# An order of steps rewritten: the quantised layer within the cross attention before it, and the first causal scores at its end

## What is computed

```
x6 = x5 + attention(norm(x5), ctx)                 # third layer: cross attention, 16 heads of 8, 77 keys
q  = clip(round(norm(x6) / s), -128, 127)          # s = max(|norm(x6)|) / 127 per token
x7 = x6 + (q @ weight_q.T) * s * weight_scale + bias      # quantised layer
y  = norm(x7)                                      # input of a decoder of four layers:
for l in range(4):                                 #   l = 0 begins here
    q, k, v = split(rmsnorm(y) @ Wqkv.T + b)       #   rope on q and k
    y += causal_attention(q, k, v) @ Wo.T + bo     #   512 x 512 scores, 16 heads of 8
    y += cross_attention(rmsnorm(y), ctx)          #   masked by token segments
    y += silu(h @ Wg.T) * (h @ Wu.T) @ Wd.T        #   h = rmsnorm(y)
x8 = x7 + rmsnorm(y)
```

## Time and profile before

| | us |
|---|---|
| median of 3 runs | 2295.73 |
| lowest and highest | 2293.84, 2301.45 |
| the profiled execution | 2289.95 |
| its span in the profile | 2288.2 |
| PE, DVE, ACT, POOL busy | 1928.6, 1443.6, 1072.7, 634.6 |
| mean granted clock of PE | 0.914 of full |

### The profile page before, as it was taken

The page is one execution under the profiler, slowest core; times in us unless marked ns, Lnnn a source line. Parts: engine busy times, 40 slices in busy tenths (PEclk is TensorE's granted clock), DMA queues, the critical chain, the costliest instruction groups (busy, mean ns, idle before and its releaser), DMA issues.

```text
span 2288.2 us, 33985 instructions
## 1 busy us (share of the span) xinstructions
PE 1928.6 (84%) x13195; PEld 1171.1 (51%) x13195; DVE 1443.6 (63%) x3533; ACT 1072.7 (47%) x1517; POOL 634.6 (28%) x858
## 2 busy tenths in 40 slices
PE   5977999675772899999889899889999989989977
PEld 4556565364541444565544465544455544456553
DVE  7546655553666777754577774477775457776468
ACT  2542555221451566454366555256645446645510
POOL 1111000322423444200354310245420144421020
PEclk9988999677785899899899899999989989989988
DMA  7001000121000000000000000000000000000000
GB/s 248 14 1 56 1 1 12 33 76 49 23 1 12 1 1 1 1 10 12 14 1 1 1 11 1 26 1 1 1 1 10 1 14 2 1 1 10 1 1 19
DMA packets 26929, 38.60 MB, mean 17 GB/s; under 512 B 5384, under 2 KB 20112, under 8 KB 26128
## 3 DMA queue, kind: packets, MB, share of 16 engines
q1 hardware_dynamic: 24720, 32.23, 4.3%
q0 software_dynamic: 2048, 4.20, 0.6%
HBM read 25.93 MB, written 10.49 MB: 16 GB/s over the span
## 4 chain that ended last, share of the span: by engine, by line
PE 45%; DVE 12%; ACT 6%; issue 4%; POOL 1%; DVEq 0%; POOLq 0%; ACTq 0%
PE wide L681 33%; PE acc L681 13%; DVE maxima L1587 4%; ACT prob L1829 3%; DVE hid L1109 1%; POOL rstd L1887 1%; DVE x L1648 1%; ACT prob L1752 1%; DVE moments L1142 1%; DVE hid L1266 1%; DVE qkv L1555 1%; ACT hn L1717 1%; DVE maxima L1275 1%; DVE hn L1187 1%; ACT q_g L1673 0%
## 5 line engine op out<-in xcount | busy, mean ns | idle before, releaser
L1587 DVE TENSOR_REDUCE maxima<-wide 128x2 f32<-128x512 f32 (+3 forms) x512 | 407.3, 819 | 167.5 <-PE wide L681 164.0
L1829 ACT ACTIVATE prob<-wide 128x768 f32<-128x768 f32 (+1 forms) x384 | 331.4, 881 | 140.4 <-PE wide L681 140.1
L1752 ACT ACTIVATE prob<-wide 77x1024 f32<-77x1024 f32 x256 | 260.2, 1019 | 150.5 <-PE wide L681 150.3
L1275 DVE TENSOR_REDUCE maxima<-wide 128x8 f32<-128x616 f32 x256 | 202.9, 795 | 174.4 <-PE wide L681 172.8
L681 PE MATMUL wide<-q_g 32*128 32x256 f32 (+3 forms) x2048 | 273.8, 403 | 33.9 <-ACT prob L1829 18.5
L2030 POOL TENSOR_SCALAR_AFFINE_SELECT prob<-prob 128x256 f32<-128x256 f32 (+1 forms) x384 | 186.5, 490 | 353.7 <-ACT prob L1829 351.2
L681 PE MATMUL wide<-q_g,kx 128*77 128x512 f32 x512 | 258.0, 576 | 3.2 <-DVE hid L1513 2.0
L1887 POOL TENSOR_TENSOR rstd<-moments,cst 128x4 f32<-128x4 f32 x88 | 89.9, 1021 | 580.9 <-DVE moments L1163 282.4
L681 PEld LDWEIGHTS wide<-q_g 32*128 32x128 f32 x2048 | 141.4, 192 | 209.5 <-issue 116.7
L1673 ACT ACTIVATE q_g<-wide 128x1024 fp32r<-128x1024 f32 x128 | 131.2, 1025 | 212.2 <-PE wide L681 212.2
L1673 ACT ACTIVATE q_g<-acc 128x512 fp32r<-128x512 f32 x192 | 114.5, 597 | 178.4 <-PE acc L681 178.0
(11 more groups left out here) (228 smaller groups left out, 3141.8 us busy)
## 6 DMA issues: line engine op xcount, KB each, us to landing
A<-in_w SPq DMA_DIRECT2D x2, 2048.0 KB, 12.9
unit_w<-in_unit_w SPq DMA_DIRECT2D x8, 448.0 KB, 3.4
ffn_w<-in_ffn_w SPq DMA_DIRECT2D x4, 768.0 KB, 4.3
slots_in<-f2x SPq DMA_DIRECT2D x1, 2560.0 KB, 23.8
prob<-slots_in SPq DMA_DIRECT2D x8, 320.0 KB, 3.1
slots_out<-A SPq DMA_DIRECT2D x8, 320.0 KB, 2.2
...
```

Source lines behind the costliest of these rows:

```text
L1275: e.tensor_reduce(maxima[g % 2][:, 2 * half:2 * half + 2, :], v, AX.X, ALU.max, negate=True).then_inc(*made("max", ("free", tile)))
L1587: e.tensor_reduce(top[:, t, h], v[:, :, at0:at0 + P * t + P], AX.X, ALU.max, negate=True).then_inc(*made("max", *([("free", tile)] if t == ...
L1752: e.activation(p[0:SC, :], s[0:SC, :], ACT.Exp, bias=0.0, scale=1.0).then_inc(*made("exp", pb, ("free", tile)))
L1829: e.activation(pv, sv, ACT.Exp, bias=0.0, scale=8 ** -0.5).then_inc(*made("exp", pb, ("free", tile)))
```

## The change

1. `clear` is cut in nine pieces (CLEARS): eight memsets of 640 columns of A and a last piece with the rest. They lie beside the scores of entry 1 of the third layer.
2. The quantised layer of entries 0 and 1 is put within the third layer's items: `stats`, `apply` and the three parts of `quantise` at the end of the phase of finish(b), and `turn`, `f2_matmul`, `stats` and `apply` of "in" in one phase more. For entry 0 `begin` of the first decoder layer follows in that phase, and `rotate`, `cut_q` and `cut_k` in another.
3. The quantised layer of entries 2 and 3 gets two phases that lie beside the causal attention's items, and so do the masks (masks3 beside item 5, mask_turn beside item 6, counted from 0).
4. `quantise` is the same nine instructions, now in three steps; f2_matmul's product has two buffers of its own (f2_hid).

```diff
+    def quantised(b):
+        quantise = [("quantise", b, k) for k in range(3)]
+        if b > 1:
+            return [[[]]] * b + [
+                in_rows((3, ("stats", "f2", 0, b)), (5, ("apply", "f2", 0, b)), *zip((7, 9, 11), quantise)),
+                in_rows((1, ("turn", "f2", 0, b)), (3, ("f2_matmul", b)), (6, ("stats", "in", 0, b)), (10, ("apply", "in", 0, b)))]
+        head = [[("stats", "f2", 0, b)], [("apply", "f2", 0, b)] + quantise]
+        tail = [[], [], [("turn", "f2", 0, b)], [("f2_matmul", b)], [("stats", "in", 0, b)], [("apply", "in", 0, b)]]
+        if b:
+            return [head, tail]
+        tail += [[("stats", "s", 0, b), ("variance", "s", 0, b)], [("apply", "s", 0, b)], [], [("turn", "s", 0, b)],
+                 [("qkv", 0, b, 0)], [("qkv", 0, b, 1), ("bias_o", 0)]]
+        return [head, tail, [[("rotate", 0, b, k)] for k in range(6)] + [[("cut_q", 0, b)], [("cut_k", 0, b)]]]
+
+    if n == 3:
+        items = [[prepare(b), scores(b), attend(b)] for b in range(B)]
+        items[1][1] = beside(items[1][1], [[("clear", k)] for k in range(CLEARS)])
+        for b, item in enumerate(items):
+            more = quantised(b)
+            item += [finish(b) + more[0]] + more[1:]
+        return items
...
     def prepare(b, g):
+        if (l, b, g) == (0, 0, 0):
+            return in_rows((11, ("qk_turn", l, b, g)))
+        if (l, b) == (0, 0) and g < 3:
+
+            return beside(in_rows((8, ("qk_turn", l, b, g))),
+                          in_rows((0, ("stats", "s", l, 1)), (2, ("variance", "s", l, 1)), (4, ("apply", "s", l, 1)),
+                                  (8, ("turn", "s", l, 1)), (10, ("qkv", l, 1, 0)), (12, ("qkv", l, 1, 1)))
+                          if g == 1 else rotate(1, *[(k, 3 * k) for k in range(5)]))
...
-    items = [[[[("stats", "f2", 0, b)], [("apply", "f2", 0, b), ("quantise", b)], [], [], [("turn", "f2", 0, b)]],
-              [[("f2_matmul", b)]], [[("stats", "in", 0, b)], [("apply", "in", 0, b)]]] for b in range(B)]
-    items[0][0] = beside(items[0][0], [[("clear",)]])
-    every += items
     for l in range(NL):
         project, rotate, items = self_steps(l)
-        every[-1] = [beside(every[-1][0], project)] + every[-1][1:]
         if l == 0:
-            items[1][0] = beside(items[1][0], [[("masks3", k)] for k in range(4)] + [[], [], [("mask_turn", "l3")]])
-        every += [rotate] + items + cross_steps(4 + l) + [[[]]]
+            items[5][0] = beside(items[5][0], in_rows(*[(3 * k, ("masks3", k)) for k in range(4)]))
+            items[6][0] = beside(items[6][0], in_rows((5, ("mask_turn", "l3"))))
+            every.append([[]])
+        else:
+            every[-1] = [beside(every[-1][0], project)] + every[-1][1:]
+            every.append(rotate)
+        every += items + cross_steps(4 + l) + [[[]]]
```

61 lines of the change are left out of this document (34 added, 27 removed).

## The result

| | runs | median us | lowest to highest |
|---|---|---|---|
| before | 10 | 2301.22 | 2289.36 to 2311.89 |
| after | 10 | 2281.72 | 2277.18 to 2294.56 |

The ratio is 0.9932, with a 95% interval of 0.9911 to 0.9953: the change makes the kernel faster by 0.7%, some 15.6 us (the two medians lie 19.5 us apart). The forecast was 31.3 us, twice what the ratio gives. The direction held, and the time lies inside the range of 2249 to 2283, near its upper end. The profiled execution of after is the slowest of its ten (2294.56 us, span 2292.8, granted clock 0.907), that of before (2289.95, 0.914) is about as fast as the fastest of its ten (2289.36), so the two profiles must not be compared by their spans, but stretch by stretch.

The account below looks back on a forecast made before the run. PE paced the causal items; ahead of them PE waited for DVE and POOL, whose chain ran in series. Terms of -55.3, +22.5 and +1.5 gave -31.3 us, from 2295.73 to 2264.4, range 2249 to 2283.

Parts of the forecast that it names:

- The main term: Ahead of the causal attention: the first causal maximum starts at 695.5 and not at 750.8, -55.3 us.
- the chain's last one: Entry 0's chain beside entry 3's attend, up to the first causal maximum: 26 us, with 20 or 32 possible.
- no wait of PE for a maximum is above 4 us: Sign near 640 us, around the scores of entries 2 and 3: no PE wait above 4 us there.
- entry 3's logits don't start near 669: Sign ahead of entry 3's attend: its logits would start near 669, as before.
- The failing step: Causal attention's items 0 to 4, now carrying moved DVE work: 82.9 us together against 60.4, +22.5.
- the masks' turn: mask_turn beside a full causal item, where PE has no idle time that covers it: +1.5 us.
- POOL: Items 1 to 4: DVE's instructions slowed beside POOL's work, taken at 3, 1, 1 and 1 us.
- The segments' wait: Item 4: DVE stands some 4 us for the segments' load, with entry 1's maxima queued behind.
- the sum: Whole kernel: -55.3, +22.5 and +1.5 give -31.3 us, from 2295.73 to 2264.4 us.
- the port rival: Causal items: all 28 moved DVE instructions cost 0.98 us extra each beside POOL, whole time 2285; chance 0.12.
- My rival: From 640 us to the sixth item: PE's clock stays at 1.2 GHz, +59 us if throughout; chance 0.05.
- the 0.8 at which I said I would be wrong: Sign in the causal items: the prediction is wrong if PE's clock there falls under 0.8.

Follow-up runs that it names:

- experiment 4: Three edits of the changed kernel: entry 1's rotation on POOL shrunk, rounding and clipping of entries 2 and 3 left out, and both; ratios 0.9928, 0.9930, 0.9926 to before.
- e10: Changed kernel with the clear as one whole memset again, at its new place beside entry 1's scores; ratio 0.9922 to the kernel before.
- experiment 6: Variants of the changed kernel with the quantised layer of entries 2 and 3 and the masks placed in other items; ratios 0.9856 to 0.9935 to before.
- e6: Changed kernel with the causal logits' products of items 1 to 5 issued twice; ratio 0.9955 to the kernel before.
- e15: Changed kernel with an own buffer for the segments, the masks over items 7 to 10 and their turn beside item 11; ratio 0.9935 to before.
- e7: Changed kernel with entry 1's rotation on POOL shrunk to 128x8 blocks; ratio 0.9928 to the kernel before.
- e5: Changed kernel, segments' own buffer, entry 2's quantised layer from the cross attention's end to item 1, entry 3's over items 2 to 5, masks over 7 to 10; ratio 0.9868.
- e11: As e5, with the masks put back into items 3 and 4 and their turn beside item 5; ratio 0.9856 to the kernel before.
- e3: Changed kernel, segments' own buffer, entry 3's quantised layer over items 3 to 6, masks over 7 to 10, their turn beside item 11; ratio 0.9888 to before.

## Why the forecast was half right

- **The main term.** -55.3 us to the first causal maximum, measured -48.9. The mechanism is as told: PE's waits of 12.69 and 19.41 us are gone, the chain of entry 0 runs beside the cross attention's end. The part that was short is the chain's last one: from 669.3 to 700.3, 31 us, where I took 26 and named 32 as the bound. POOL's timeline shows most of it: 20.4 us from rotation to cut, where I had 17.2, because POOL stood 2.83 us for DVE's f_hid, for which I had 2.3, and 1.47 for DVE's x, for which I had nothing. Another 1.1 us each lie ahead of the rotation (6.5 instead of 5.4) and behind the cut (4.1 instead of 3.0). In the scores of entries 2 and 3 no wait of PE for a maximum is above 4 us (the longest is 3.2), as forecast. But entry 3's logits don't start near 669: they start at 674.92, behind entry 0's input projection (669.06 before).
- **The failing step: the items.** Forecast 82.9 us for items 0 to 4 and 12 for item 5, against 92.4 and 15.9 (means of after's two profiles 92.2 and 15.9). I took DVE's work from the earlier trace rows, added the new work, and let it pace, with 1 or 2 us for waits, and left PE's clock as it was before (0.85 in item 0, 1.00 from item 2 on). The term was 24.0 us with the masks' turn, and 36.6 were measured. For item 1 it held in size (16.0 and 16.4), though that item, too, is DVE's run and then PE's at the lower level (experiment 4). For the others it didn't, for these reasons:
  - Item 0: 15.1 instead of 12.5. PE is busy for 13.63 of it at 0.74, with 10.05 of DVE. I had put PE's clock at 0.85; at 0.79 (e10) the item takes 14.3.
  - Item 2: 17.2 instead of 14.6. DVE is busy for 14.05, where I had 12.6 and 1 for POOL, and stands 3.2 us; entry 1's projection and norm alternate with PE's products at 0.69. At 0.90, in the second profile, the item takes 16.3 with the same DVE work, so 0.9 us of the 2.6 are the clock's.
  - Items 3 and 4: 43.7 instead of 39.8. The segments' wait was right at 4.75 us, but lies at the end of item 3, as the first piece of the masks stands ahead of item 4's first maximum. To it come 1.7 us of wait for POOL's root, and, as I read experiments 4 and 6, DVE's run and PE's in series rather than one engine's total; this last is argued and not shown by itself.
  - Item 5: 15.9 instead of 12.0. It has little of the moved work, and DVE only 7.54 us. PE ends it, busy for 15.58 us at 0.68, and e6 adds 3.3 us to this item. Items 5 and 11 both take 10.5 us in the kernel before, and with the masks' turn and a clock of 0.68 both take 15.9 (item 11 of e15, experiment 6). So 2.5 us are the turn's, where I had 1.5, and 2.9 the clock's, for which I had nothing.
- **POOL.** 6 us in the sum. DVE's three groups above are busy for 11.3 us. Four such norms alone take 1.11 us and a rounding 0.43 (e7), which makes 5.3 for the 16 norms and two roundings: 6.0 us over that. The term was right, and the port rival (+21) far too dear.
- **The masks' turn.** +1.5 in the sum; 2.5 us at the full clock in item 11 (e5), and 1.3 in item 5 of e11 (13.1 us, where e5 has 11.8 without it, both at 1.00).
- **The clock.** My rival had a price of 59 us and a fall of the whole stretch to the lower level. It fell to 0.59 to 0.82 in items 0 to 5, below the 0.8 at which I said I would be wrong, and cost far less, since in most of them PE isn't the only pace: 1.1 us for 0.64 instead of 0.79 in items 1 and 2. In items 0 and 5, PE's, it costs what it says, 2.9 us in item 5. To put it at nothing in the sum was a mistake. The row at 0.68 that I gave for "busy for less than half" was misread: it is item 1 of the earlier trace rows, where PE is busy for 10.20 of 10.80 us. The clock's whole part in the missing 20 us isn't settled.
- **What the sum could not see.** Its method, DVE's new total per item plus a small wait, charges a heap of work like the same work spread thin. e3 and e5 show the difference: the same instructions in other items are worth 7 us (e15 to e3), with the clock's share in it, and e5's stretch is 27.2 us below before's first profile and 34.1 below its second. The 31 us that I forecast were there, by another arrangement. That the measured time lies inside the range is owed to the range's width, not to the items' sum.
